# Causal scores of a two-state attention as 64-row tiles, with running states for the blocks under the diagonal

## What is computed

```python
z = jax.lax.cumlogsumexp(s, axis=2)
g = jnp.exp(jnp.concatenate([z[:, :, :1], z[:, :, :-1]], axis=2) - z)
p = jnp.exp(s - z)
...
    hk = hk * g_t[:, :, None, :] + k_t[..., None] * p_t[:, :, None, :]
    return (hk, jnp.einsum('bhk,bhkm->bhm', q_t, hk))
...
pvT = jax.nn.softmax(okT, axis=-1)
...
    hv = hv * g_t[..., None] + p_t[..., None] * v_t[:, :, None, :]
    return (hv, jnp.einsum('bhm,bhmv->bhv', pv_t, hv))
```

## Time and profile before

| | us |
|---|---|
| median of 3 runs | 2246.0 (2242.24 to 2246.45) |
| the profiled execution, its own time | 2245.59 |
| its span, first to last instruction | 2243.9 |
| TensorE busy | 2121.0 (95%) |
| VectorE busy | 1546.9 (69%) |
| ScalarE busy | 989.9 (44%) |
| GpSimd busy | 547.6 (24%) |

### The profile page before, as it was taken

One profiled execution on the slowest core, in us unless ns is written; L12 is line 12 of the kernel. 1 busy time (PEld: TensorE's weight loads), 2 busy tenths in 40 slices (PEclk: granted clock), 3 DMA queues, 4 the chain that ended last, 5 costly groups with the idle time before them and its releaser, 6 DMA issues. The chain is left out here.

```text
span 2243.9 us, 32513 instructions
## 1 busy us (share of the span) xinstructions
PE 2121.0 (95%) x11316; PEld 1560.7 (70%) x11316; DVE 1546.9 (69%) x2451; ACT 989.9 (44%) x2026; POOL 547.6 (24%) x630
## 2 busy tenths in 40 slices
PE   7999999999999999999999968999999979999996
PEld 5788878888787887888888754434333358778785
DVE  4776767767677676676767848888788645555547
ACT  3443443434444344443444423777777742111210
POOL 3142251242242143142332222212121011111111
PEclk9999999999999999999999976999999989999998
DMA  4000100100001001001000000000000010000002
GB/s 150 1 1 11 34 10 1 33 10 19 16 10 34 1 11 34 1 11 34 1 10 1 1 4 7 14 14 19 9 16 10 2 29 29 14 28 14 28 14 75
DMA packets 56039, 42.60 MB, mean 19 GB/s; under 512 B 13936, under 2 KB 46704, under 8 KB 55920
## 3 DMA queue, kind: packets, MB, share of 16 engines
q1 hardware_dynamic: 55920, 40.92, 5.9%
HBM read 32.78 MB, written 4.19 MB: 16 GB/s over the span
## 5 line engine op out<-in xcount | busy, mean ns | idle before, releaser
L1251 DVE TENSOR_REDUCE x_nm<-x_ps 128x1 f32<-128x512 f32 x512 | 327.9, 685 | 72.7 <-PE x_ps L1062 67.7
L1228 ACT ACTIVATE x_prob<-x_ps 128x1024 f32<-128x1024 f32 x256 | 261.6, 1028 | 93.3 <-PE x_ps L1080 91.7
L1062 PE MATMUL x_ps<-x_ks,x_qs 64*128 64x512 f32 x512 | 223.5, 501 | 8.9 <-DVE x_nm L1251 8.2
L356 POOL TENSOR_TENSOR a_causal<-a_causal,a_mask 128x128 f32<-128x128 f32 x128 | 68.3, 545 | 593.0 <-ACT a_causal L618 591.5
L64 PE MATMUL a_ps<-a_vg_hi,a_xT_lo 128*128 128x512 f32 x512 | 209.3, 409 | 2.1 <-DVE a_vg_lo L810 2.1
L1062 PEld LDWEIGHTS x_ps<-x_ks,x_qs 64*128 64x128 f32 x512 | 90.3, 195 | 171.0 <-DVE x_nm L1251 136.1
L66 PE MATMUL a_ps<-a_vg_hi,a_xT_hi 128*128 128x512 f32 x512 | 200.4, 391 | 0.0
L65 PE MATMUL a_ps<-a_vg_lo,a_xT_hi 128*128 128x512 f32 x512 | 200.1, 391 | 0.0
L469 PE MATMUL a_ps<-a_right_hi,a_left 128*128 128x256 f32 (+2 forms) x512 | 164.6, 338 | 22.0 <-issue 16.8
L1080 PE MATMUL x_ps<-x_qs,x_ks 64*128 64x512 f32 x512 | 179.1, 454 | 0.9 <-ACT x_prob L1228 0.8
L596 ACT CAST a_right_hi<-a_og 64x512 fp32r<-64x512 f32 x128 | 79.2, 619 | 194.1 <-DVE a_og L784 191.7
(11 more groups left out here) (158 smaller groups left out, 4618.6 us busy)
## 6 DMA issues: line engine op xcount, KB each, us to landing
a_raw_vg<-in_L_attn_Wv_dram SPq DMA_DIRECT2D x8, 512.0 KB, 4.2
a_raw_vg<-in_L_attn_Wg_dram SPq DMA_DIRECT2D x8, 512.0 KB, 6.3
a_raw_qks<-in_L_attn_Wo_dram SPq DMA_DIRECT2D x8, 512.0 KB, 3.5
out_dram<-acc SPq DMA_DIRECT2D x8, 512.0 KB, 3.3
x_xrows<-acc SPq DMA_DIRECT2D x13, 256.0 KB, 2.8
acc<-in_x_dram SPq DMA_DIRECT2D x3, 1024.0 KB, 9.7
f_raw_down<-in_L_ffn_down_w_dram SPq DMA_DIRECT2D x11, 256.0 KB, 2.9
f_raw_gu<-in_L_ffn_gate_w_dram SPq DMA_DIRECT2D x11, 256.0 KB, 2.9
```

The costliest lines, as they stand in the source:

```text
L1062: pe.matmul(max_bank(u, i, par), qs[HALF[par], q, tile, st * P:(st + 1) * P], ks[HALF[par], q, tile // 2, :], start=True, stop=True).then_ ...
L1228: nc.scalar.activation(prob[:, s % 4, :, :], exb[s % 2], ACT.Exp, scale=X_SCALE)\
L1251: nc.vector.tensor_reduce(nm[:, q % 2, i % 4, par, i // 4:i // 4 + 1], max_bank(u, i, par), AX.X, ALU.max, negate=True).then_inc(max_read, 1)
```

## The change

1. The scores are computed from tiles of 64 rows. `left_hi`, `left_lo`, `right_hi`, `right_lo` keep the layout of the projections, head 0 in rows 0 to 63 and head 1 in rows 64 to 127. Each block takes three products (hi lo, lo hi, hi hi) for each head, the two heads in turn. ScalarE and VectorE make each of the four with one operation on 128 rows.
2. The second use of the scores (w e^T) computes only the four diagonal blocks, 128 wide (`diagonals`), which VectorE masks in two operations. What lies under the diagonal comes from states: e^T v of each block of 128 tokens (`states`, after the transposes of `pv`), summed by VectorE (`running_states`), and multiplied by w in `values`.
3. `values` then has 8 products of the diagonal blocks and 6 with the states, fills ob[0] with head 0 and ob[1] with head 1, and signals `o_done` once, at its end.
4. In `chunks`, block 3 is 128 wide and lies in chunk 1, so chunk 2 is block 2 alone. ScalarE copies head 0 of chunks 0 and 1, VectorE copies and masks head 1 of them and both heads of chunk 2. Chunk 2 waits for ScalarE's first copy and for VectorE's first.

```diff
-CHUNKS = [[(0, 0, 0)], [(1, 0, P)], [(3, P, 2 * P), (2, 0, 2 * P)]]
+CHUNKS = [[(0, 0, 0)], [(1, 0, P), (3, 3 * P, 3 * P)], [(2, 0, 2 * P)]]
...
+            def blocks(banks, i, col, first, last):
+                out = slice(col, col + last - first)
+                for h in range(2):
+                    pe.matmul(banks[h][:, out], left_lo[HALF[h], i * P:(i + 1) * P], right_hi[HALF[h], first:last],
+                              start=True, stop=False)
...
+            def chunks(n):
+                wait(pe, diag_masked, n)
                 for c in range(3):
+                    if c == 2:
+                        pe.wait_ge(chunk_act, 2 * n + 1)
+                        pe.wait_ge(chunk_dve, 4 * n + 1)
+                    for i, col, first in CHUNKS[c]:
+                        mm = blocks((okb, tb) if c == 1 else ch, i, col, first, T)
+                    mm.then_inc(chunk_done, 1)
+
+            def diagonals(n):
+                for i in range(TT):
+                    mm = blocks(ch, i, i * P, i * P, (i + 1) * P)
+                mm.then_inc(diag_done, 1)
+
+            def states(n, j):
+                pe.wait_ge(v_ready, 4 * n + 4)
+                for i in range(TT - 1):
                     for h in range(2):
+                        mm = pe.matmul(tb[HALF[h], i * P:(i + 1) * P], e[:, i, DK * h:DK * (h + 1)],
+                                       v[:, j % 2, i, h * DV:(h + 1) * DV], start=True, stop=True)
+                mm.then_inc(states_done, 1)
...
             def values(n, j):
+                pe.wait_ge(diag_masked, n + 1)
                 wait(pe, added, 4 * n)
                 for t in range(TT):
                     for h in range(2):
-                        for i in range(t + 1):
-                            at = KEY_AT[i] + (t - i) * P
-                            c = (2 * (t % 2) + h) * P
-                            mm = pe.matmul(ob[t // 2][:, c:c + P], causal[:, h, at:at + P],
-                                           v[:, j % 2, i, h * DV:(h + 1) * DV], start=(i == 0), stop=(i == t))
-                    if t % 2:
-                        mm.then_inc(o_done, 1)
+                        pe.matmul(ob[h][:, t * P:(t + 1) * P], causal[:, h, t * P:(t + 1) * P],
+                                  v[:, j % 2, t, h * DV:(h + 1) * DV], start=(t == 0), stop=False,
+                                  skip_group_check=True)
+                pe.wait_ge(state_ready, 3 * n + 3)
+                for t in range(1, TT):
+                    for h in range(2):
+                        mm = pe.matmul(ob[h][:, t * P:(t + 1) * P], wT[HALF[h], t * P:(t + 1) * P],
+                                       state[HALF[h], t - 1, :], start=False, stop=True, skip_group_check=True)
+                mm.then_inc(o_done, 1)
...
             def high_right(src):
-                for h in range(2):
-                    for half in (h, 1 - h):
-                        nc.scalar.copy(right_hi[HALF[half], h, :], src[HALF[h], :]).then_inc(right_hi_ready, 1)
+                nc.scalar.copy(right_hi[:, :], src).then_inc(right_hi_ready, 1)
...
                 for half in range(2):
-                    act.wait_ge(o_done, 2 * n + half + 1)
-                    for g in range(4):
-                        sq = nc.scalar.activation(squares[:, 4 * half + g, 0:DV],
...
+                    act.wait_ge(o_done, n + 1)
+                    for t in range(TT):
+                        g = 2 * t + half
+                        sq = nc.scalar.activation(squares[:, g, 0:DV], ob[half][:, t * P:(t + 1) * P], ACT.Square,
```

More of the change, by code:

```diff
@@ L322, in _ @@
                                     pattern=[[-1, P]], channel_multiplier=1).then_inc(const_ready, 1)
[L324 removed]
+            for m in (0, 3):
                 nc.gpsimd.affine_select(out=mask[:, m, :], in_=mask[:, m, :], compare_op=ALU.is_ge, fill=0.0,
@@ L455, in project @@
                 mm.then_inc(proj_done, 1)
-            def chunks(n, which):
-                for c in range(3):
-                    for h in range(2):
[L461 to L473, removed]
+            def blocks(banks, i, col, first, last):
[4 more added lines that the diff above has]
+                for h in range(2):
+                    pe.matmul(banks[h][:, out], left_hi[HALF[h], i * P:(i + 1) * P], right_lo[HALF[h], first:last],
+                              start=False, stop=False)
+                for h in range(2):
+                    mm = pe.matmul(banks[h][:, out], left_hi[HALF[h], i * P:(i + 1) * P], right_hi[HALF[h], first:last],
+                                   start=False, stop=True)
+                return mm
@@ L551, in step @@
                     .then_inc(pvT_done, 1)
+                states(n, j)
                 next_project(VG + 2, VG + 3)
-                pe.wait_ge(left_ready, 2 * (2 * n) + 4)
-                pe.wait_ge(right_ready, 2 * (2 * n) + 4)
+                pe.wait_ge(left_ready, 2 * n + 2)
+                pe.wait_ge(right_ready, 2 * n + 2)
                 if at(n, 0) or at(n, 1):
                     pe.wait_ge(xlo_ready, (n + 3) * KT)
-                chunks(n, 1)
+                diagonals(n)
                 next_project(Q, K)
@@ L589, in high_left @@
             def high_left(src):
-                for h in range(2):
-                    nc.scalar.copy(left[HALF[h], h, :], src[HALF[h], :]).then_inc(left_hi_ready, 1)
+                nc.scalar.copy(left_hi[:, :], src).then_inc(left_hi_ready, 1)
             def high_right(src):
-                for h in range(2):
-                    for half in (h, 1 - h):
-                        nc.scalar.copy(right_hi[HALF[half], h, :], src[HALF[h], :]).then_inc(right_hi_ready, 1)
+                nc.scalar.copy(right_hi[:, :], src).then_inc(right_hi_ready, 1)
             def copy_proj(m, i, b):
@@ L613, in copy_proj, with copy_chunks @@
                                          scale=0.5).then_inc(tanh_ready, 1)
-            def copy_chunk0(n, which):
-                for h in range(2):
-                    wait(act, chunk_done, 12 * n + 6 * which + h + 1)
-                    nc.scalar.copy(causal[:, h, 0:CHUNK_LEN[0]], ch[h]).then_inc(chunk_act, 1)
+            def copy_chunks(n):
+                act.wait_ge(chunk_done, 3 * n + 1)
+                nc.scalar.copy(causal[:, 0, 0:T], ch[0]).then_inc(chunk_act, 1)
+                act.wait_ge(chunk_done, 3 * n + 2)
+                nc.scalar.copy(causal[:, 0, CHUNK_AT[1]:CHUNK_AT[1] + T], okb).then_inc(chunk_act, 1)
             def copy_oT(n):
```

129 lines of the change are left out of this document (72 added, 57 removed).

## The result

| kernel | median us | runs (range) | ratio to before, 95% interval | profiled execution, span |
|---|---|---|---|---|
| before | 2244.1 | 4 (2242.2 to 2246.5) | | 2245.6, 2243.9 |
| after | 2257.6 | 4 (2255.5 to 2265.0) | 1.0059 [1.0041, 1.0077] | 2265.0, 2263.2 |

The change makes the kernel 0.6% slower, where 1.3% faster was forecast.

What follows compares the result with a forecast made beforehand. TensorE, busy 39.35 of 39.70 us a step, was taken as the bound. Thirty steps (-20.7 us), the first (4.4) and the last (3.2) save 28.3 us from the profiled 2245.6: 2217 forecast, range of all cases 2202 to 2270.

Steps and rivals of the forecast that it cites:

- The sum: Change per regular step of TensorE's program: -1.83 + 0.90 - 0.88 + 1.12 = -0.69 us, for steps of 39.0 us.
- The rival: A 2 us stall in each step could lower TensorE's clock; a half-clock step some 38 us longer; 2260 and above; chance 0.05.
- `values` -1.83: Products of diagonal blocks and states in each step: 2.55 us instead of 4.38, if 64-row pairs run together.
- `states` +0.90: Six added products with 64 output rows per step: three pairs of two records, 0.9 us with edges.
- Diagonal blocks -0.88: Second scores in each step: 12 pairs at 0.112 us plus edges, 1.75 us instead of 2.63.
- the rival of 0.22 us: Narrow 128-wide float32r pairs at float32's rate: 1.3 us more in each of 32 steps, 2259 in all; chance 0.32.
- First score to `slots` +1.12: Late squares stall TensorE about 2 us before chunk 2; `slots` starts at about 7.33 us against 6.21.
- the forecast's own range: Total time if the main forecast of 2217 holds: 2206 to 2232 us.
- The returns: Six ways back of the loop, 2.2 us idle each, keep the stall because VectorE's copy comes later there too.
- The first step: Shorter wait for the first `left` (-1.35), no squares ahead of chunks (-1.3); with the other three terms -4.4 us.
- The last step: Operand copies -2.7, `values` and second scores -3.3, squares take back 1.0 there and 1.8 before `slots`: -3.2 us.
- The range: Total time over all cases, 2202 to 2270 us, including narrow pairs at float32's rate and part of the clock.

## Why the prediction was wrong

**The failed step is the clock.** The sum has no term for it: the stall is priced at its own length, as if the matmuls behind it ran at full speed. The trace of after shows a half-clock piece behind 19 of 22 such stalls and 25 pieces in the attention, 1.5 us each, some 38 us in all. The rival was named, with the right mechanism and place (a stall of 2 us in each step), though it reckoned with whole steps at half clock, 38 us each, and not with short pieces in nearly all of them. It was given 0.05, on the ground that 2.2 us of idle at the loop's return left the clock at 1.00. Five returns stood against some thirty stalls that the change would add, and the table shows that an idle time of that length lowers the clock in most cases and not in every one. The kernel before has ten returns of 1.7 to 2.3 us in two profiles without one loss; that made the ground look firmer than it was, and why it is spared is not shown (its `values` of 4.4 us ahead of the return is one candidate). By the Trainium skill, "TensorE: Matmul & The Clock Gate", section "HAM oscillation — how this bites in real kernels", a wait repeated in each pass can cost the clock in each pass; the steps of after agree, 19 of 22. The waits told of there are longer ones, for DMA; here stalls of 2.0 to 2.2 us did it.

**The steps.** By PE's timelines of undisturbed steps, forecast and measured, us per step: `values` -1.83 and -1.82. `states` +0.90 and +1.09 (0.80 and dearer starts ahead of it and in the projections behind). Diagonal blocks -0.88 and -1.00 (they take 1.49 us instead of 2.61, and Q and K behind them 0.12 more): 0.11 us a pair, as taken, and the rival of 0.22 us, chance 0.32, is out. First score to `slots` +1.12 and +1.24 (7.43 to 7.48 against the 7.33 forecast). The sum is -0.49 against -0.69, steps of 39.2 us against 39.0. The stall was forecast at 2 us, ended by VectorE's copy, and is 2.17, ended by it. So the terms held within 0.2 us each, and over 30 steps they give 6 us less than forecast.

**The clock's term.** The 25 pieces, at 1.5 us each, are some 38 us. Without them the profiled execution would stand near 2227, within the forecast's own range. That is worked out; the runs that keep everything else and take the stall away confirm it in the steps (39.2 us in each with three or seven extra matmuls). Their totals, 2241 and 2249, stay above that, since their returns of the loop became dearer (42 to 46 us).

**The returns.** They were said to keep the stall. In after, undisturbed ones cost 0.4 to 0.8 us over a regular step (39.6 to 40.0 against 39.2), in before 1.4 to 1.9, since ScalarE's and VectorE's late work now runs while TensorE is idle for its return. That is some 5 us better than forecast. (The trace shows five such returns and a sixth was counted.)

**The first step** was forecast at -4.4, of which -2.65 (1.35 and 1.3) lie ahead of its `slots`; there +2.9 was measured. "No squares stand ahead of its chunks" was true, but something else does:

```profile
43.20 1.70 DVE L744 RECIPROCAL a_rz<-a_rz 128x256 f32<-128x256 f32 x1
44.81 1.22 DVE L750 TENSOR_TENSOR a_causal<-a_ps,a_mask 128x512 f32<-128x512 f32 x2
45.59 0.39 PE L469 MATMUL a_ps<-a_right_hi,a_left_lo 64*128 64x256 f32 x2 [3.35 <-DVE a_causal L750]
```

Chunk 0 of head 1 was ScalarE's before and is VectorE's now, and in the first step VectorE has a scan and two reciprocals of 1.7 us queued ahead of it. TensorE waits 3.35 us, and S behind it runs at half clock. The first scores start at 40.47 instead of 41.00, 0.5 earlier where 1.35 was forecast.

**The last step** was forecast at -3.2, of which -5.0 lie behind the start of its `slots` (-2.7, -3.3 and +1.0); there -0.7 was measured. The way from w to its operands gave its 2.7: the second scores start 3.07 us behind the transposes of `pv` instead of 5.79. But `values` took longer than before, 5.34 us instead of 4.70: behind a wait of 3.17 us for VectorE's masks nearly all of it ran at half clock (the 16 records below take 3.7 us, 1.9 in a regular step):

```profile
1330.89 3.78 PE L540 MATMUL a_ps<-a_v,a_causal 128*128 128x128 f32 x16 [3.17 <-DVE a_causal L758]
1334.60 1.63 PE L546 MATMUL a_ps<-a_state,a_og 64*128 64x128 f32 x12
```

That wait also left little of the gain in the second scores (4.73 us to the start of `values` instead of 5.18), and the wait for GpSimd's scaling behind `values` is 7.14 us instead of 6.04.

The range, 2202 to 2270, held the time, since it took in part of the clock; the sign and the predicted time were wrong. That the measured 2257.6 lies next to the 2259 of the rival with the dear narrow pairs is chance: a pair costs 0.11 us, not 0.22.

## What to carry to other kernels

An engine that is 95% busy can afford a new wait only if its clock can. Sum up not only the time of a new stall but the length of each single one, put it beside all idle times of that length in the trace, and count how often they are allowed to happen: a few harmless ones prove nothing for thirty. If the work can't be made shorter, split a neighbouring block of independent matmuls around the wait, which here turned a loss of 0.6% into a gain of 1.2%, and into 2.4% with the chain on the other engines shortened.

## What the runs showed of the hardware that I had not expected

- Idle times of 0.6 to 1.3 us lowered the clock in 1 of 193 cases, those of 1.9 to 2.3 us in 34 of 52. Two of 1.1 and 1.0 us, 3.5 us apart, were harmless.
- Matmuls on 64 of 128 rows kept the clock up in a stall as those on 128 rows did (39.2 us steps in both fills).
- Pairs of float32r matmuls of 64 rows and 128 columns, each with its own weights, start 0.11 us apart.
- At the loop's return idle times of 2.1 to 2.3 us lowered the clock in 0 of 5 cases with the longer `values` ahead of them (4.4 us) and in 14 of 17 with the shorter one (2.6 us).
- TensorE stands still for 1.7 to 2.8 us at each return of the hardware loop, with no wait that explains it. With sixteen more float32 matmuls (3.84 us) in every fourth step a second stop of 0.7 to 1.7 us came 2.7 to 3.2 us behind the first.
